# The second attention of a fused two-layer block, rewritten: queries and keys stacked along the partitions, heads' keys packed in chunks, all batches unrolled

## Chip, cores and metric

The kernel runs on one NeuronCore of a Trainium2 chip. The metric is the device time of one launch in microseconds. Three runs of the kernel before the change gave 1285.15, 1285.19 and 1286.05 us; the median is 1285.19 us.

## What is computed

Sixteen batches of 256 tokens by 256 channels (x) pass through two layers. Each layer is a cross attention on a context of 77 rows, and then a feed-forward part. The change is in the second attention:

```
x = x + L0_xattn(layernorm(x), ctx)      # 16 heads of 64, shared key and value, causal
x = x + L0_ffn(layernorm(x))
x = x + L1_xattn(layernorm(x), ctx)      # 16 heads of 16
x = x + L1_ffn(layernorm(x))             # soft mixture of 16 experts

# L1_xattn(x_q, x_kv):
q = x_q @ w_q;  k, v = split(x_kv @ w_kv)          # 16 heads of 16 channels
logits = q.k * 16**-0.5 + (query position - key position) * w_rel[head]
out = softmax(logits) @ v                          # per head, over 77 keys
return out @ w_proj
```

All is fp32. For a product that has to be exact to fp32, an operand is split into a rounded part (`_hi`, of type fp32r) and the rest (`_lo`), and three matmuls (hi·hi, hi·lo, lo·hi) replace one.

## The kernel before

The program is written by hand for each engine; semaphores order the engines, and each engine runs its own list in order. The stages follow one another with a barrier between them: `prologue` (keys and values of both layers from the context, for all batches, kept in SBUF), `attention(0)`, `ffn`, `attention(1)`, `moe`.

`attention` (line 328) serves both layers. For the second one a batch has 8 steps t, one for a pair of heads. GpSimd lays the keys of the batch out so that each head's 16 channels stand on their own partitions with zeros elsewhere (`lay_out_keys`, L733), and the values too (`lay_out_values`, L745 and L747). In step t, TensorE computes the scores of the pair for both halves of the queries: for each half a bf16 matmul that adds the position bias (L484) and an fp32 matmul of 128 x 154 (L486), which the trace shows as two records. VectorE takes the row maxima (`find_maxima`, L641), ScalarE the exponentials (L610), VectorE the sums and inverses (L646, L651), and GpSimd multiplies them (L770). A step later in the same batch loop, for the batch before, TensorE transposes the pair's 2 x 2 blocks of probabilities (L496, four transposes, each of 128 columns of which 77 are a head's keys), ScalarE and VectorE split them (L588, L674), and TensorE weighs the values (L510, six matmuls). In the last part of a batch the heads are projected (L522) and added to x (L684), and the next batch's x is transposed (L451) and multiplied by the query weights (L462). The batches 2 to 14 are one hardware loop (`loop`, L405), and its body has two batches in flight.

SyncE (SP) issues nothing within a batch. Its work in this stage is at the start: three loads of constants and six small copies from SBUF to SBUF that bring the bias rows to their partitions (L427 to L434).

Of the kernel before, what the change touches and what calls it, by code (L numbers as in the profile page):

```python
# [117 lines left out]
def prologue(nc, d, st):  # L118
# [9 lines left out]
    with ExitStack() as stack:  # L128
# [22 lines left out]
        def _(sp):  # L151
# [71 lines left out]
        def _(act):  # L223
# [6 lines left out]
            for t, (out, lo, hi) in enumerate(((wk[0][:, :, 0:DK0], 0, DK0), (wk[0][:, :, DK0:P], 0, DK0),  # L230
# [12 lines left out]
            for g in range(GROUPS):  # L243
                if g < GROUPS - 1:
                    transposed_ctx(g + 1)
                for k in range(G):
                    act.wait_ge(val_psum, g * G + k + 1)
                    nc.scalar.copy(st.val0[0:SK, bass.ds(g * G + k, 1), :], val_ps[k % 2][0:SK, 0:DK0].unsqueeze(1))
                    nc.scalar.copy(st.val1[0:SK, bass.ds(g * G + k, 1), :],
                                   val_ps[k % 2][0:SK, DK0:VC].unsqueeze(1)).then_inc(val_done, 1)  # L250

        @block.vector
        def _(dve):
            for t, (i, a, b, lo, hi) in enumerate(((wk, 0, DK0, 0, DK0), (wk, DK0, P, 0, DK0),
# [4 lines left out]
                op = nc.vector.tensor_tensor(i[1][:, :, a:b], w_raw[:, :, lo:hi], fp32_of(i[0][:, :, a:b]), ALU.subtract)  # L259
# [68 lines left out]
def attention(nc, d, st, index):  # L328
# [6 lines left out]
    with ExitStack() as stack:  # L335
        m = Memory(nc, stack, f"att{index}")
        L0 = index == 0
        dk = DK0 if L0 else DK1
# [13 lines left out]
        KC = 1 if L0 else CH  # L352
        KH = 2 if L0 else HC
# [6 lines left out]
        vals = m.split("vals", [P, (2 if L0 else H) * P + HC * dk])  # L360
# [8 lines left out]
        if L0:  # L369
            ident16 = m.sb("ident16", [P, P], BF16)  # L370
            causal_raw = m.sb("causal_raw", [P, PAIR])
            causal16 = m.sb("causal16", [P, PAIR], BF16)
        else:

            pos_raw = m.sb("pos_raw", [P, N])
            pos16 = m.sb("pos16", [P, N], BF16)

            w_rel = m.sb("w_rel", [H, 1])
            neg_k = m.sb("neg_k", [H, SK])
            slope = m.sb("slope", [H, 2, SK])  # L380
            part = m.sb("part", [H, 2, SK])
            part16 = m.sb("part16", [H, 3, 2, SK], BF16)
            bias16 = m.sb("bias16", [P, H, SK], BF16)

# [7 lines left out]
        bias_in, vals_zero = m.sem("bias_in"), m.sem("vals_zero")  # L392
        c_in, c_ready, zeroed, c_step = m.sem("c_in"), m.sem("c_ready"), m.sem("zeroed"), m.sem("c_step")
# [48 lines left out]
        def _(pe):  # L442
# [1207 lines left out]
```

## Time and profile before

| | us |
|---|---|
| median of three runs | 1285.19 |
| profiled execution, from its first to its last instruction (span) | 1284.3 |
| TensorE busy | 1155.0 (90%) |
| VectorE busy | 946.6 (74%) |
| ScalarE busy | 744.9 (58%) |
| GpSimd busy | 443.5 (35%) |
| DMA traffic | 18.63 MB, mean 15 GB/s |

The device time of the profiled execution itself is not given beside its span. The span is 0.9 us below the median of the runs, and the prediction adds these 0.9 us to a span to get a time. Times within the profile are counted from the first instruction. Busy time is a union of an engine's instructions, so it can't tell alone whether the engine is the bound: for that one looks at what it waited for. The names in the rows leave out the index of the stage and of the buffer, so `att_s_bank` stands for both attentions; the second attention is the stretch from 696.7 to 1032.3 us.

### The profile page before, as it was taken

What the parts mean: (1) busy time and instruction counts of PE and PEld (TensorE: products, weight loads), DVE (VectorE), ACT (ScalarE), POOL (GpSimd) and SP (SyncE); (2) the same over time, 40 slices, a digit from 0 to 9 for tenths busy, and PEclk for the clock granted to TensorE, in tenths of its full rate; (3) what the DMA queues carried; (4) which work ended last, traced back from release to release, by engine and by line L of the source; (5) the groups of instructions that cost most, each with busy time, mean ns of one, the idle gap of its engine ahead of it and who ended that gap; (6) DMA issues with size and microseconds to landing.
All of it is one profiled execution on the core that took longest, in us unless ns stands there. A gap on an engine that the chain in (4) does not pass through costs nothing. (4 is left out here: it accounts for less than half of the span.)

```text
span 1284.3 us, 31779 instructions
## 1 busy us (share of the span) xinstructions
PE 1155.0 (90%) x9045; PEld 1104.0 (86%) x9045; DVE 946.6 (74%) x2439; ACT 744.9 (58%) x2297; POOL 443.5 (35%) x656
## 2 busy tenths in 40 slices
PE   7689999999999987999996799999999947767998
PEld 7689999999999987999996699999999837767777
DVE  3567777677776666777776688888888659997656
ACT  3466677567765654333332577677677516666754
POOL 0232222322322210221213454554555346664015
PEclk9889999999999998999998799999999968999559
DMA  7010000000000001000000000000000000000103
GB/s 239 23 67 1 0 0 0 0 0 0 0 0 0 0 2 29 1 0 0 0 0 4 2 1 0 0 0 0 0 0 0 1 18 1 1 0 1 39 27 123
DMA packets 20583, 18.63 MB, mean 15 GB/s; under 512 B 6620, under 2 KB 19644, under 8 KB 20412
## 3 DMA queue, kind: packets, MB, share of 16 engines
q1 hardware_dynamic: 19724, 17.45, 4.3%
q10 hardware_dynamic: 816, 0.66, 0.2%
q8 instruction: 21, 0.34, 0.1%
q14 instruction: 22, 0.18, 0.0%
HBM read 13.89 MB, written 4.19 MB: 14 GB/s over the span
## 5 line engine op out<-in xcount | busy, mean ns | idle before, releaser
L770 POOL TENSOR_TENSOR att_prob<-att_ex,att_rinv 128x308 f32<-128x308 f32 x256 | 179.8, 705 | 326.1 <-DVE att_rinv L651 290.6
L610 ACT ACTIVATE att_ex<-att_s_bank,att_mx 128x77 f32<-128x77 f32 x1024 | 250.2, 334 | 17.1 <-DVE att_mx L641 15.2
L674 DVE TENSOR_TENSOR att_pT_lo<-att_t_bank,att_pT_hi 128x512 fp32r<-128x512 f32 x256 | 176.6, 690 | 50.4 <-ACT att_pT_hi L588 48.1
L486 PE MATMUL att_s_bank<-att_keys,att_qT 128*128 128x154 f32 x1024 | 205.5, 315 | 0.0
L588 ACT CAST att_pT_hi<-att_t_bank 128x512 fp32r<-128x512 f32 x256 | 150.0, 587 | 75.2 <-PE att_t_bank L496 70.3
L510 PE MATMUL att_o_bank<-att_pT_hi,att_vals_hi 128*128 128x256 f32 x512 | 167.5, 327 | 5.1 <-DVE att_pT_lo L674 2.9
L486 PEld LDWEIGHTS att_s_bank<-att_keys,att_qT 128*128 128x128 f32 x1024 | 152.7, 194 | 6.7
L496 PE MATMUL att_t_bank<-all_ident,att_prob 128*128 128x128 f32 x1024 | 152.9, 272 | 0.0
L510 PE MATMUL att_o_bank<-att_pT_lo,att_vals_hi 128*128 128x256 f32 x512 | 144.1, 281 | 0.0
L510 PE MATMUL att_o_bank<-att_pT_hi,att_vals_lo 128*128 128x256 f32 x512 | 143.9, 281 | 0.0
L618 ACT ACTIVATE att_qT<-att_q_bank 128x256 f32<-128x256 f32 x160 | 61.6, 385 | 136.9 <-PE att_q_bank L462 135.9
L893 ACT ACTIVATE ffn_hid<-ffn_h_bank,ffn_b 128x256 f32<-128x256 f32 x128 | 60.7, 476 | 125.6 <-DVE ffn_hT_lo L924 63.0
L641 DVE TENSOR_REDUCE att_mx<-att_s_bank 128x4 f32<-128x308 f32 x256 | 120.0, 469 | 16.8 <-PE att_s_bank L486 16.8
L646 DVE TENSOR_REDUCE att_rsum<-att_ex 128x4 f32<-128x308 f32 x256 | 118.2, 462 | 1.7 <-ACT att_ex L610 1.2
L496 PEld LDWEIGHTS att_t_bank<-all_ident,att_prob 128*128 128x128 f32 x1024 | 118.1, 140 | 0.0
L510 PEld LDWEIGHTS att_o_bank<-att_pT_hi,att_vals_hi 128*128 128x128 f32 x512 | 96.7, 189 | 9.3 <-DVE att_pT_lo L674 6.5
L462 PE MATMUL att_q_bank<-att_xT_hi,att_wq_hi 128*128 128x256 f32 x320 | 96.1, 300 | 4.9 <-DVE att_xT_lo L634 4.9
L655 DVE TENSOR_TENSOR att_oT_lo<-att_o_bank,att_oT_hi 128x256 fp32r<-128x256 f32 x160 | 67.8, 424 | 40.4 <-ACT att_oT_hi L623 36.6
L510 PEld LDWEIGHTS att_o_bank<-att_pT_lo,att_vals_hi 128*128 128x128 f32 x512 | 96.7, 189 | 0.0
L510 PEld LDWEIGHTS att_o_bank<-att_pT_hi,att_vals_lo 128*128 128x128 f32 x512 | 96.3, 188 | 0.0
L462 PE MATMUL att_q_bank<-att_xT_hi,att_wq_lo 128*128 128x256 f32 x320 | 91.9, 287 | 0.0
L462 PE MATMUL att_q_bank<-att_xT_lo,att_wq_hi 128*128 128x256 f32 x320 | 91.5, 286 | 0.0
(215 smaller groups left out, 3363.0 us busy)
## 6 DMA issues: line engine op xcount, KB each, us to landing
all_x<-in_x SPq DMA_DIRECT2D x4, 1024.0 KB, 8.1
out<-comb_y SPq DMA_DIRECT2D x16, 256.0 KB, 2.1
all_raw<-in_L_ffn_w SPq DMA_DIRECT2D x2, 1024.0 KB, 5.8
moe_w_raw<-in_L_ffn_w SPq DMA_DIRECT2D x32, 64.0 KB, 2.1
pro_ctx_in<-in_ctx SPq DMA_DIRECT2D x4, 308.0 KB
all_raw<-in_L_xattn_W_q SPq DMA_DIRECT2D x1, 1024.0 KB, 8.2
all_raw<-in_L_xattn_W_o SPq DMA_DIRECT2D x1, 1024.0 KB, 10.7
pro_w_raw<-in_L_xattn_w_kv ACTq DMA_DIRECT2D x1, 512.0 KB, 4.8
```

The source lines that it names most:

```text
L462: last = nc.tensor.matmul(q_bank[c % 2][:, 0:N], wq[a][:, k, c * P:(c + 1) * P], xT[b][:, k, :], start=n == 0, stop=n == 5)
L486: last = nc.tensor.matmul(out, qT[c % 2][:, q * P:(q + 1) * P], keys[:, kc, h0:h0 + 2, :], start=first, stop=True)
L496: last = nc.tensor.transpose(t_bank[t % 2][:, h * N + q * P:h * N + (q + 1) * P], prob[:, q, (2 * t + h) * SK:(2 * t + h) * SK + P], st.id ...
L510: last = nc.tensor.matmul(o_bank[j % 2][:, 0:N], vals[a][:, v * P:(v + 1) * P], pT[t % 2][b][:, h * N:(h + 1) * N], start=t % PC == 0 and ...
L588: nc.scalar.copy(pT[t % 2][0][:, :], t_bank[t % 2][:, :]).then_inc(pt_hi, 1)
L610: last = nc.scalar.activation(ex[t % RING][:, r, :], s_bank[t % 2][:, r * SK:(r + 1) * SK], ACT.Exp, bias=mx[t % 2][:, r:r + 1])
L618: nc.scalar.mul(qT[c % 2][:, :], q_bank[c % 2][:, 0:N], scale).then_inc(q_ready, 1)
L641: nc.vector.tensor_reduce(mx[t % 2][:, :], s_bank[t % 2][:, 0:NC * PAIR].rearrange("p (r k) -> p r k", k=SK), AX, ALU.max, negate=True).th ...
L646: nc.vector.tensor_reduce(rsum[t % RING][:, :], ex[t % RING][:, :, :], AX, ALU.add).then_inc(sum_ready, 1)
L655: nc.vector.tensor_tensor(oT[1][:, j, :], o_bank[j % 2][:, 0:N], fp32_of(oT[0][:, j, :]), ALU.subtract).then_inc(ot_lo, 1)
L674: nc.vector.tensor_tensor(pT[t % 2][1][:, :], t_bank[t % 2][:, :], fp32_of(pT[t % 2][0][:, :]), ALU.subtract).then_inc(pt_lo, 1)
L770: nc.gpsimd.tensor_tensor(out, e, w, ALU.mult).then_inc(p_ready, 1)
```

## The change

`attention` becomes two functions. `attention0` does what it did for the first layer. `attention1` is new code for the second:

- **Scores.** Queries and keys are kept as stacks: `qs` has the 16 channels of both heads of a pair three times along the partitions (hi, lo, hi; 96 rows) and four rows with positions and ones, `ks` the keys in the same way (hi, hi, lo) and four bias rows. One fp32r matmul over 100 rows replaces the bias matmul and the fp32 matmul. The scale is folded into the key weights in `prologue`.
- **How the stacks get there.** DMAs from SBUF to SBUF, issued by SyncE: per batch 12 for the queries (`load_queries`), 24 for the keys (`load_keys`) and 20 for the values (`load_values`). `lay_out_keys` is gone; `lay_out_values` multiplies the copied values by a mask, in four GpSimd instructions.
- **Probabilities.** The first 64 keys of a pair of heads fill one 128-column chunk, and the last 13 keys of eight heads fill a 104-column chunk. So a batch has five units of four transposes and six value matmuls in place of eight.
- **Order.** All batches are unrolled into stages f = -2 to 17. In stage f run the scores of batch f, the transposes and values of batch f-1 and the projection of batch f-2, and the queries of batch f+1.
- **prologue.** It splits keys and values of the second layer into hi and lo for all batches (two more ScalarE casts per group of four batches, one more VectorE subtraction per batch).

The core of the diff, with eight columns of indent taken away:

```diff
-def attention(nc, d, st, index):
+def attention0(nc, d, st):
...
+def attention1(nc, d, st):
...
+BIAS, ROWS = 96, 100
...
+qs = [m.sb(f"qs{i}", [P, HP, N], F32R) for i in range(2)]
+ks = [m.sb(f"ks{i}", [P, DC, 4, 2, SK], F32R) for i in range(2)]
+vd = [m.split(f"vd{i}", [P, D]) for i in range(2)]
+vt = [m.split(f"vt{i}", [P, D]) for i in range(2)]
+vmain = [m.split(f"vmain{i}", [P, HP * 160]) for i in range(2)]
+vtail = [m.split(f"vtail{i}", [P, DC, P]) for i in range(2)]
...
+prob = m.sb("prob", [P, NC, HP * P])
+tails = [m.sb(f"tails{i}", [P, NC, 2 * TAILS]) for i in range(2)]
+pT = [m.split(f"pT{i}", [P, 2 * N]) for i in range(2)]
...
+QS_DMAS, KS_DMAS, V_DMAS = 12, 24, 20
+VALS = 4
+STAGES = range(-2, B + 2)
+UNIT_AT = {0: 0, 1: 1, 3: 2, 4: 3, 6: 4}
+CHUNKS = {0: (0, 1), 1: (2, 3), 2: (4, 5), 4: (6, 7)}
+TAIL_UNIT = 3
...
+    sp.dma_start(w_rel[:, :], d["L1_xattn_w_rel"].rearrange("a h -> h a")).then_inc(c_in, 16)
+    sp.dma_start(neg_k[:, :], d["neg_k"]).then_inc(c_in, 16)
+    sp.dma_start(pos_raw[BIAS:ROWS, :], d["positions"]).then_inc(c_in, 16)
+    def load_queries(f):
+        i = f % 2
+        sp.wait_ge(q_lo, f + 1)
+        at_least(sp, s_psum, HP * (f - 1))
+        for k, part in enumerate((0, 1, 0)):
+            for r in range(4):
+                sp.dma_start(fp32_of(qs[i][32 * k:32 * k + 32, :, :]).rearrange("p (c r) n -> p c r n", c=DC)[:, :, r, :],
+                             fp32_of(qT[part][32 * r:32 * r + 32, :, :])).then_inc(qs_in[i], 16)
+    def load_keys(f):
+        i = f % 2
+        at_least(sp, s_psum, HP * (f - 1))
+        for k, part in enumerate((0, 0, 1)):
+            for r in range(4):
+                for h in range(2):
+                    a = 32 * r + DK1 * h
+                    sp.dma_start(fp32_of(ks[i][32 * k + DK1 * h:32 * k + DK1 * h + DK1, :, r, h, :]),
+                                 fp32_of(st.key1[part][a:a + DK1, :, f, :])).then_inc(ks_in[i], 16)
+    def load_values(f):
+        i = f % 2
+        at_least(sp, vals_ready, VALS * (f - 1))
+        for part in range(2):
+            v = fp32_of(st.val1[part][:, f, :])
+            for h in range(2):
+                sp.dma_start(fp32_of(vd[i][part][MAIN * h:MAIN * h + MAIN, :]), v[0:MAIN, :]).then_inc(v_in[i], 16)
+            for h in range(8):
+                sp.dma_start(fp32_of(vt[i][part][TAIL * h:TAIL * h + TAIL, :]), v[MAIN:SK, :]).then_inc(v_in[i], 16)
+    load_values(0)
+    sp.wait_ge(ks_zero, 2)
+    load_keys(0)
+    load_keys(1)
+    load_values(1)
+    sp.wait_ge(c_step, 4)
+    for i in range(2):
+        for r in range(2):
+            for part in range(2):
+                row = BIAS + 2 * r + part
+                sp.dma_start(fp32_of(ks[i][row:row + 1, :, :, :, :]).rearrange("p c r h k -> p (c r h) k"),
+                             fp32_of(bias[part][:, r, :])).then_inc(bias_in, 16)
+    for f in range(B):
+        load_queries(f)
+        if 1 <= f < B - 1:
+            load_keys(f + 1)
+            load_values(f + 1)
...
+    def scores(f, t):
+        i = f % 2
+        if t == 0:
+            pe.wait_ge(qs_in[i], 16 * QS_DMAS * (f // 2 + 1))
+            pe.wait_ge(ks_in[i], 16 * KS_DMAS * (f // 2 + 1))
+        if t == 0 and f < 2:
+            pe.wait_ge(bias_in, 128)
+            pe.wait_ge(pos_ready, 2)
+        at_least(pe, ex_ready, HP * f + t - 1)
+        for q in range(NC):
+            last = nc.tensor.matmul(s_bank[t % 2][:, q * PAIR:(q + 1) * PAIR], qs[i][0:ROWS, t, q * P:(q + 1) * P],
+                                    ks[i][0:ROWS, t // 4, t % 4, :, :], start=True, stop=True)
+        last.then_inc(s_psum, 1)
+    def transpose_p(g, u):
+        n = UNITS * g + u
+        pe.wait_ge(p_ready, probs_of(g, u))
+        at_least(pe, pt_lo, n - 1)
+        for j in range(2):
+            for q in range(NC):
+                at = j * N + q * P
+                if u == TAIL_UNIT:
+                    last = nc.tensor.transpose(t_bank[n % 2][0:TAILS, at:at + P],
+                                               tails[g % 2][:, q, j * TAILS:(j + 1) * TAILS], st.ident[:, :])
+                else:
+                    t = CHUNKS[u][j]
+                    last = nc.tensor.transpose(t_bank[n % 2][:, at:at + P],
+                                               prob[:, q, t * P:(t + 1) * P], st.ident[:, :])
...
+    for f in STAGES:
+        for t in range(HP):
+            if here(f):
+                scores(f, t)
+            if here(f - 1) and t in UNIT_AT:
+                transpose_p(f - 1, UNIT_AT[t])
+            if t == 0 and here(f - 2):
+                weigh_values(f - 2, 4)
+            if t == 0 and here(f + 1):
+                transpose_x(f + 1)
+            if t == 2 and here(f + 1):
+                queries(f + 1)
+            if here(f - 1) and t in (2, 3, 5, 6):
+                weigh_values(f - 1, {2: 0, 3: 1, 5: 2, 6: 3}[t])
+            if t == 4 and here(f - 2):
+                project(f - 2)
...
+    def round_queries(f):
+        act.wait_ge(q_psum, f + 1)
+        at_least(act, qs_in[(f - 1) % 2], 16 * QS_DMAS * ((f - 1) // 2 + 1))
+        nc.scalar.copy(qT[0][:, :, :], xq_bank[:, :].rearrange("p (c n) -> p c n", c=DC)).then_inc(q_hi, 1)
...
+    def weigh(f, t):
+        n = HP * f + t
+        pool.wait_ge(inv_ready, n + 1)
+        if f > 0 and t % 2 == 0:
+            pool.wait_ge(t_psum, UNITS * (f - 1) + unit_of(t) + 1)
+        e = ex[t % RING][:, :, :].rearrange("p (q h) k -> p q h k", q=NC)
+        w = rinv[t % RING][:, :].rearrange("p (q h) -> p q h", q=NC).unsqueeze(3)
+        main = prob[:, :, t * P:(t + 1) * P].rearrange("p q (h k) -> p q h k", h=2)
+        tail = tails[f % 2][:, :, t * 2 * TAIL:(t + 1) * 2 * TAIL].rearrange("p q (h k) -> p q h k", h=2)
+        nc.gpsimd.tensor_tensor(main, e[:, :, :, 0:MAIN], w.to_broadcast([P, NC, 2, MAIN]), ALU.mult).then_inc(p_ready, 1)
+        nc.gpsimd.tensor_tensor(tail, e[:, :, :, MAIN:SK], w.to_broadcast([P, NC, 2, TAIL]), ALU.mult).then_inc(p_ready, 1)
...
+        pool.wait_ge(v_in[i], 16 * V_DMAS * (g // 2 + 1))
+        at_least(pool, pv_done, UNITS * (g - 1))
+        for part in range(2):
+            main = vmain[i][part][:, :].rearrange("p (t n) -> p t n", n=160)[:, :, 0:2 * DK1]
...
@@ prologue
-        for j in range(3):
-            dve.wait_ge(key_psum, g * 3 + j + 1)
...
-            nc.vector.tensor_copy(out, keys).then_inc(key_done, 1)
...
+        for k in range(G):
+            dve.wait_ge(val1_hi, g * G + k + 1)
+            nc.vector.tensor_tensor(st.val1[1][0:SK, bass.ds(g * G + k, 1), :],
+                                    val_ps[k % 2][0:SK, DK0:VC].unsqueeze(1),
+                                    fp32_of(st.val1[0][0:SK, bass.ds(g * G + k, 1), :]), ALU.subtract).then_inc(val_done, 1)
```

The list of SyncE at the start of the second attention, before (the names are destination<-source, then the shape of the destination):

```order
L427 DMA att_w_rel<-in_L_xattn_w_rel 16x1
L428 DMA att_neg_k<-in_neg_k 16x77
L429 DMA att_pos_raw<-in_positions 128x256
L434 DMA att_bias<-att_part 1x16x77 x6
```

After these the list before has nothing until the next stage. The same place of the changed kernel, first the rows that stand ahead of the first queries:

```order
L839 DMA att_pos_raw<-in_positions 4x256
L866 DMA att_vd_hi<-kv_val_hi 64x256 x2
L868 DMA att_vt_hi<-kv_val_hi 13x256 x8
L866 DMA att_vd_lo<-kv_val_lo 64x256 x2
L868 DMA att_vt_lo<-kv_val_lo 13x256 x8
L857 DMA att_ks<-kv_key_hi 16x2x77 x16
L857 DMA att_ks<-kv_key_lo 16x2x77 x8
L857 DMA att_ks<-kv_key_hi 16x2x77 x16
L857 DMA att_ks<-kv_key_lo 16x2x77 x8
```

and then, for one batch in the middle of the stage, what SyncE has to issue each time:

```order
L847 DMA att_qs<-att_qT_hi 32x2x256 x4
L847 DMA att_qs<-att_qT_lo 32x2x256 x4
L847 DMA att_qs<-att_qT_hi 32x2x256 x4
L857 DMA att_ks<-kv_key_hi 16x2x77 x16
L857 DMA att_ks<-kv_key_lo 16x2x77 x8
L866 DMA att_vd_hi<-kv_val_hi 64x256 x2
L868 DMA att_vt_hi<-kv_val_hi 13x256 x8
L866 DMA att_vd_lo<-kv_val_lo 64x256 x2
L868 DMA att_vt_lo<-kv_val_lo 13x256 x8
```

These are 12 + 24 + 20 = 56 DMAs; before there were none in a batch. On TensorE, one step of the loop before, for a pair of heads:

```order
L496 MATMUL att_t_bank<-all_ident,att_prob 128x128 x4
L484 MATMUL att_s_bank<-att_bias,att_pos 128x154
L486 MATMUL att_s_bank<-att_keys,att_qT 128x154
L484 MATMUL att_s_bank<-att_bias,att_pos 128x154
L486 MATMUL att_s_bank<-att_keys,att_qT 128x154
L510 MATMUL att_o_bank<-att_pT_hi,att_vals_hi 128x256
L510 MATMUL att_o_bank<-att_pT_lo,att_vals_hi 128x256
L510 MATMUL att_o_bank<-att_pT_hi,att_vals_lo 128x256
L510 MATMUL att_o_bank<-att_pT_hi,att_vals_hi 128x256
L510 MATMUL att_o_bank<-att_pT_lo,att_vals_hi 128x256
L510 MATMUL att_o_bank<-att_pT_hi,att_vals_lo 128x256
```

and in the changed kernel the end of a stage's step t = 0 and its steps t = 1 and 2, as far as the first query matmul:

```order
L961 MATMUL att_o_bank<-att_pT_hi,att_vmain_hi 128x256
L961 MATMUL att_o_bank<-att_pT_lo,att_vmain_hi 128x256
L961 MATMUL att_o_bank<-att_pT_hi,att_vmain_lo 128x256
L900 MATMUL att_xq_bank<-all_ident,att_xn 128x128 x4
L924 MATMUL att_s_bank<-att_ks,att_qs 128x154 x2
L940 MATMUL att_t_bank<-all_ident,att_prob 128x128 x4
L924 MATMUL att_s_bank<-att_ks,att_qs 128x154 x2
L910 MATMUL att_xq_bank<-att_xT_hi,att_wq_hi 128x256
```

Two score matmuls stand where four (six records in the trace) stood, and the scores of a stage's first step wait for the DMAs of `qs` and `ks` (`scores`, t == 0), with all else of that stage behind them on TensorE.

## Rows read from the trace of the kernel before

**Rows 1.** Windows: busy of each engine, start, steady part, last batch; granted clock in shares.

```profile
core 0: us, PE busy (x) PEld busy (x) DVE busy (x) ACT busy (x) POOL busy (x), PEclk, DMA share, GB/s
841.68:860.84 19.16, 18.88 (x159) 18.10 (x157) 16.52 (x45) 13.72 (x46) 10.21 (x17) 1.00 0.00 0
...
708.00:714.00 6.00, 3.62 (x15) 2.88 (x15) 2.08 (x5) 1.13 (x3) 0.00 (x0) 0.50 0.03 4
...
1190.00:1248.00 58.00, 53.86 (x214) 44.47 (x215) 34.90 (x102) 38.67 (x99) 2.55 (x2) 0.50 0.12 32
```

**Rows 2.** Timeline of ScalarE: the same cast in three batches, one per batch.

```profile
841.68 0.65 ACT L578 CAST att_xT_hi<-att_q_bank 128x256 fp32r<-128x256 f32 x2 [0.28 <-PE att_q_bank L451]
...
860.84 0.65 ACT L578 CAST att_xT_hi<-att_q_bank 128x256 fp32r<-128x256 f32 x2 [0.27 <-PE att_q_bank L451]
...
880.01 0.65 ACT L578 CAST att_xT_hi<-att_q_bank 128x256 fp32r<-128x256 f32 x2 [0.26 <-PE att_q_bank L451]
```

**Rows 3.** Timeline of TensorE, one steady step: start, duration, what.

```profile
848.90 0.46 PEld L496 LDWEIGHTS att_t_bank<-all_ident,att_prob 128*128 128x128 f32 x4
...
849.33 0.10 PEld L484 LDWEIGHTS att_s_bank<-att_bias,att_pos 128*128 128x128 bf16 x1
...
850.05 0.19 PEld L510 LDWEIGHTS att_o_bank<-att_pT_hi,att_vals_hi 128*128 128x128 f32 x1
...
850.80 0.46 PEld L496 LDWEIGHTS att_t_bank<-all_ident,att_prob 128*128 128x128 f32 x4
```

**Rows 4.** Groups by line and shape, 725 to 1010 us: busy, mean ns, idle before.

```profile
L674 DVE TENSOR_TENSOR att_pT_lo<-att_t_bank,att_pT_hi 128x512 fp32r<-128x512 f32 x118 | 81.5, 691 | 13.0 <-ACT att_pT_hi L588 11.1
...
L733 POOL TENSOR_TENSOR att_keys<-kv_key,all_head_mask 128x616 f32<-128x616 f32 x30 | 36.7, 1222 | 0.0
```

**Rows 5.** Timeline of SP, start of the program: issues back to back.

```profile
1.22 0.38 SPq L153 DMA_DIRECT2D all_ident<-in_ident  x1
1.65 0.43 SPq L154 DMA_DIRECT2D all_head_mask<-in_head_mask  x1
2.12 0.43 SPq L155 DMA_DIRECT2D all_head_mask<-in_head_mask  x1
...
15.82 0.31 SPq L165 DMA_DIRECT2D pro_ctx_in<-in_ctx  x1
```

**Rows 6.** Timeline of SP in the second attention: all that it issues there.

```profile
696.72 0.35 SPq L427 DMA_DIRECT2D att_w_rel<-in_L_xattn_w_rel  x1
697.12 0.41 SPq L428 DMA_DIRECT2D att_neg_k<-in_neg_k  x1
697.58 0.41 SPq L429 DMA_DIRECT2D att_pos_raw<-in_positions  x1
708.08 3.79 SPq L434 DMA_DIRECT2D att_bias<-att_part  x6
```

**Rows 7.** The six copies of L434: duration min/median/max, first and last start, landing.

```profile
L434 SPq DMA_DIRECT2D att_bias<-att_part x6: 585/589/630, 708.1 to 711.3; - x6
...
DMA to landing us min/median/max: 1.8/1.8/2.1
```

**Rows 8.** Timeline of SP after 1033 us: the first and last of nine back to back.

```profile
1033.26 0.36 SPq L1051 DMA_DIRECT2D route_gamma<-in_L_ffn_ln_gamma  x1
...
1037.72 1.09 SPq L1337 DMA_DIRECT2D moe_w_raw<-in_L_ffn_w  x1
```

**Rows 9.** The line that loads 64x256 floats: duration min/median/max of 16.

```profile
L1337 SPq DMA_DIRECT2D moe_w_raw<-in_L_ffn_w x16: 480/490/1091, 1036.5 to 1231.3; - x16
```

**Rows 10.** Timeline: the first scores, the last batch's first transposes, the last addition.

```profile
713.12 0.29 PE L484 MATMUL att_s_bank<-att_bias,att_pos 128*128 128x154 bf16 x1 [0.68 <-DMA att_bias<-att_part]
...
1017.32 1.04 PE L496 MATMUL att_t_bank<-all_ident,att_prob 128*128 128x128 f32 x8
...
1028.18 0.69 DVE L674 TENSOR_TENSOR att_pT_lo<-att_t_bank,att_pT_hi 128x512 fp32r<-128x512 f32 x1 [0.45 <-ACT att_pT_hi L588]
...
1031.90 0.42 DVE L684 TENSOR_TENSOR all_x<-att_q_bank,all_x 128x256 f32<-128x256 f32 x1
```

**Rows 11.** Part 3 of the page: a queue's packets, MB, share of 16 engines.

```profile
q1 hardware_dynamic: 19724, 17.45, 4.3%
```

**Rows 12.** Groups by line: the casts of the values in the prologue.

```profile
L249 ACT COPY kv_val<-pro_val_ps 77x256 f32<-77x256 f32 x16 | 5.9, 371 | 0.0
```

More of the change, by code:

```diff
@@ L44 @@
 LN_EPS = 1e-5
+MAIN, TAIL = 64, SK - 64
+TAILS = 8 * TAIL
 PASSES = ((0, 0), (0, 1), (1, 0))
@@ L243, in _ @@
             for g in range(GROUPS):
+                for c in range(DC):
+                    act.wait_ge(key_psum, g * 3 + c + 2)
+                    nc.scalar.copy(st.key1[0][:, c, bass.ds(g * G, G), :],
+                                   key_ps[c + 1][:, 0:GK].rearrange("p (b k) -> p b k", b=G)).then_inc(key1_hi, 1)
                 if g < GROUPS - 1:
@@ L258, in _ @@
                 dve.wait_ge(w_hi, t + 1)
-                op = nc.vector.tensor_tensor(i[1][:, :, a:b], w_raw[:, :, lo:hi], fp32_of(i[0][:, :, a:b]), ALU.subtract)
+                if t == 2:
+                    for c in range(DC):
+                        op = nc.vector.scalar_tensor_tensor(i[1][:, c, a:b], w_raw[:, c, lo:hi], DK1 ** -0.5,
+                                                            fp32_of(i[0][:, c, a:b]), ALU.mult, ALU.subtract)
+                else:
+                    op = nc.vector.tensor_tensor(i[1][:, :, a:b], w_raw[:, :, lo:hi], fp32_of(i[0][:, :, a:b]), ALU.subtract)
                 if t == 2:
@@ L368, in attention @@
         oT = m.split("oT", [P, CH, N])
[L369 to L383, printed above, removed]
+        ident16 = m.sb("ident16", [P, P], BF16)
+        causal_raw = m.sb("causal_raw", [P, PAIR])
+        causal16 = m.sb("causal16", [P, PAIR], BF16)
         q_bank = [m.ps(f"q_bank{i}") for i in range(2)]
@@ L477, in scores @@
                     first = True
-                    if L0 and q == 0:
+                    if q == 0:
                         nc.tensor.matmul(out, ident16[:, :], causal16[:, :], start=True, stop=False)
-                        first = False
-                    if not L0:
-                        nc.tensor.matmul(out, pos16[:, q * P:(q + 1) * P], bias16[:, 2 * t:2 * t + 2, :], start=True, stop=False)
                         first = False
@@ L724, in _ @@
             ln.inverse_deviation(pool, 0)
-            if not L0:
-                pool.memset(bias16[:, :, :], 0.0).then_inc(zeroed, 1)
             def lay_out_keys(f, c):
@@ L1604, in build @@
         st.head_mask0 = m.sb("head_mask0", [P, 2])
-        st.head_mask1 = m.sb("head_mask1", [P, 8])
+        st.tail_mask = m.sb("tail_mask", [P, H])
         with ExitStack() as kv_stack:
             kv = Memory(nc, kv_stack, "kv")
-            st.key0 = kv.sb("key0", [P, B, SK])
-            st.key1 = kv.sb("key1", [P, DC, B, SK])
-            st.val0 = kv.sb("val0", [P, B, DK0])
-            st.val1 = kv.sb("val1", [P, B, D])
-            prologue(nc, d, st)
-            attention(nc, d, st, 0)
+            st.key1 = kv.split("key1", [P, DC, B, SK])
+            st.val1 = kv.split("val1", [P, B, D])
+            with ExitStack() as kv0_stack:
+                kv0 = Memory(nc, kv0_stack, "kv0")
+                st.key0 = kv0.sb("key0", [P, B, SK])
+                st.val0 = kv0.sb("val0", [P, B, DK0])
+                prologue(nc, d, st)
+                attention0(nc, d, st)
             ffn(nc, d, st)
-            attention(nc, d, st, 1)
+            attention1(nc, d, st)
         moe(nc, d, st, out)
```

361 lines of the change are left out of this document (295 added, 66 removed).

## The prediction

> **What bounds the kernel now.** I read the windows first, to see which engine fills a batch of the second attention. Between two casts of the same line, 19.17 us apart in each of the batches shown [rows 2], TensorE is busy 18.88 of 19.16 us, VectorE 16.52, ScalarE 13.72 and GpSimd 10.21, at the full granted clock [rows 1]. TensorE never waits long there, so it is the bound, and VectorE is only 2.6 us behind. The timeline then gives TensorE's step for a pair of heads: it starts every 1.90 us, with 0.43 us for four transposes, 0.72 us for the scores and 0.75 us for the values [rows 3]. Eight steps are 15.2 us; the other 4.0 us of a batch are x's transposes, queries and projection. The stage's first scores start at 713.12 us and its last addition begins at 1031.90 and takes 0.42, so it ends at 1032.3 [rows 10]. SyncE's first issue is at 696.72 [rows 6].
>
> Last I read SP's own timeline, because the change puts 56 DMAs per batch on a queue that had none. SP issues one after another, and each issue occupies it: 0.38 and 0.43 us, 0.43 to 0.47 us from start to start [rows 5]; 0.40 and 0.46 us in the second attention [rows 6]; 8 intervals in 4.46 us, 0.56 us each, after 1033 us [rows 8]; the form 64x256, which the values have, takes 0.49 us itself [rows 9]. The only copies from SBUF to SBUF are six of the bias: 0.59 us each in the median, (711.3 - 708.1) / 5 = 0.64 us apart, and landing 1.8 us after issue [rows 7].
>
> **TensorE's saving.** Transposes go from 8 groups of 0.43 us to 5, values from 8 of 0.75 to 5: -3.5 us. The scores were 8 x 0.72 = 5.8 us. No row has an fp32r matmul of 154 columns. At the pace of the value matmuls (0.75 / 6 = 0.125 us, with more columns) 16 of them take 2.0 us; at the pace of now, as if fp32r bought nothing, 5.8. TensorE's batch becomes 11.9 us (up to 15.7). I take 11.9, since the value matmuls have the same type.
>
> **The others.** VectorE loses three subtractions of 0.69 us [rows 4] and gains one for the queries: 16.52 - 1.4 = 15.1 us. GpSimd loses two key layouts of 1.22 us [rows 4] and gets four smaller instructions for values and a second multiplication per pair; it had 9 us free. Nothing here would exceed 16 us, so by the compute engines alone a batch would take about 16 us instead of 19.2.
>
> **What the change adds: 56 issues.** They stand in one list on SP: 12 for the queries of f, then 24 for the keys and 20 for the values of f+1. The first scores of a batch wait for its queries; the queries' copies can't be issued before the keys and values ahead of them in SP's list are. Call c the time from one issue to the next. A batch then takes 56c. To hide behind 19.2 us of work c would have to be 0.34 us, and behind 16 us it would have to be 0.28. The ends for c are 0.36 (the shortest issue, 0.31 us [rows 5], plus the 0.05 us between two) and 0.64 (the bias copies). Below 0.36 no row supports it. The bias copies are nearest in kind, but they gather 16 partitions into one, which the 56 don't do; the loads nearest in shape give 0.47 (plain) and 0.54 (64x256: 0.49 + 0.05). I take the middle, c = 0.50. A batch is then 28.0 us. Waits of SP: q_lo(f) comes about 6.5 us into stage f-1, and SP reaches the queries of f some 20 us into it, so SP doesn't wait in the steady part; the wait of the keys for the scores of the batch before last is long over as well. Two buffers don't help: the list is serial and full.
>
> The DMA engines themselves carry it: 19724 packets took 4.3% of 16 engines' span [rows 11], 45 ns each, and 56 DMAs have 12x64 + 24x32 + 4x64 + 16x13 = 2000 pieces, 2000 x 45 / 16 = 5.6 us per batch.
>
> **The sum**, on the profiled execution's clock:
> - Start: SP issues its three constants until 698.1. Then 88 copies for keys and values of two batches, 44.0 us; 8 bias copies of 0.64, 5.1 us; 12 for the queries, 6.0; landing 1.8. First scores at 755.0 instead of 713.1. The memsets of `ks` and the weights' split lie beside it.
> - Batch 1: its queries wait for q_lo, three steps of 1.9 and a split after the first scores, 761.5; issued by 767.5. The keys of batch 2 wait until the scores of batch 0 are over, seven steps, 768.3; then 44 issues, 22 us: 790.3.
> - Thirteen periods of 28.0 us: the queries of batch 15 start at 1154.3; + 6.0 + 1.8: its scores start at 1162.1.
> - Tail: stage 15 runs free, 8 x 1.9 = 15.2 us. Stage 16 has five units, and the last batch now needs (1032.3 - 1017.3) / 8 = 1.9 us for each of eight [rows 10]: 9.4. Stage 17 is the last values, head, projection and addition, now 4.1 us from 1028.18 on [rows 10]. End at 1190.8 against 1032.3: +158.5 us.
> - Prologue: 16 more subtractions on VectorE, and a bank of the values is released only after a cast (0.37 us [rows 12]) and a subtraction. It lengthens the values by about 0.15 us each, +2 us, of a bound of 0 (under the loads) to 6.
> The later stages are unchanged. Span 1284.3 + 160.5 = 1444.8 us, plus the 0.9 us by which the median lies above the span: 1446 us. Of c the sum depends by 88 + 12 + 44 + 13x56 + 12 = 884 issues: 0.01 us in c is 8.8 us in the kernel.
>
> The Trainium skill (DMA: Bandwidth & Descriptors, "Why a DMA increments its semaphore by 16 and not by 1") gives 512 sequencer cycles for a DMA instruction on chips of this generation, and its first page (Trainium Kernel Development and Optimization, "NeuronCore Architecture") 1.2 GHz for SyncE: an estimate of 0.43 us, by which the sum would be 1384 us. The back-to-back rows of 0.43 to 0.47 agree with it roughly, the bias rows don't.
>
> **TensorE's clock** falls in two stretches: 0.50 at the stage's start, where TensorE had stood, and 0.50 also in the experts, although busy 53.86 of 58 us [rows 1]. With 12 of 28 us busy I expect stretches at 1.2 GHz. At that level the 11.9 us of a batch become 24, still below 28; had the scores cost their upper end, 15.7 would be 31 and the batches would take 3 us more: about +45 us.
>
> **Rivals.**
> - *Issues are cheap, compute bounds (faster).* If short copies with fixed addresses take SP under 0.317 us, the kernel is faster, since (1446 - 1285) / 884 = 0.183 below 0.50 is where the gain begins; from 0.28 down VectorE sets the pace. At c = 0.25 the first scores are at about 730, fifteen stages of 16 us follow, the tail adds 29: 999 instead of 1032, 1255 us with the prologue. For it: one isolated issue of 0.31. Against it: it was isolated, and the closest pair shown is 0.40 us apart [rows 6]. The Trainium skill (same page, "Issuing engines are not separate DMA queues") calls an issuer's time usually small relative to the DMA itself; by that rule this rival is the one to expect. The trace doesn't agree: 0.59 us of issue stand against 1.8 us to landing [rows 7]. Chance 0.07.
> - *Short issues, still the bound.* c from 0.32 to 0.39, as the isolated issues of 0.31 to 0.35 plus the gap: at 0.36, 1322 us. Chance 0.10.
> - *All copies cost like the bias copies.* c = 0.64, 35.8 us per batch: 1446 + 884 x 0.14 = 1570 us. For it: they are the only rows from SBUF to SBUF, the first of them took 0.63 us after a pause, and in the run of nine an issue took 1.09 [rows 8], so a long list may be slower than a short one. Chance 0.08.
>
> **Numbers.** My forecast, SP's list as the bound with c between 0.39 and 0.63, has 0.75. The range is from c = 0.39 (1349) to the neighbourhood of 0.63 (1561), with TensorE's clock within it: 1350 to 1560. A measurement of this kernel tells 0.2%, 2.6 us, from no change. Faster by more: 0.07. Within it c would have to be 0.314 to 0.320: 0.01. Slower: the rest, 0.75 + 0.10 + 0.08 less that 0.01, 0.92. The range leaves out the low rival for the most part, the faster one and half of the high one.
>
> **What would show it.** SP in the second attention: some 900 issues from end to end without a wait from 698 us to about 1160; TensorE waiting at each first scores for `qs`, 10 us or more per batch; a period of 56 issues, the same batch after batch; PE's clock below 1 there; scores' matmuls at half of before. I am wrong if SP waits in its list for q_lo or for the scores, or if its issues are under 0.32 us, and wrong in size if they are not about 0.50.

## The result, and the profile after

| | before | after |
|---|---|---|
| median | 1285.17 us (4 runs) | 1624.99 us (4 runs, 1623.41 to 1627.62) |
| ratio | | 1.264, 95% interval 1.262 to 1.266 |
| span of the profiled execution | 1284.3 us | 1621.3 us |
| second attention: SyncE's first issue to the end of the last addition | 696.7 to 1032.3 | 699.3 to 1370.6 |
| from there to the last instruction | 252.0 | 250.7 |

The forecast was 1446 us, in 1350 to 1560. The direction and the mechanism were right; the size was not, and the time lies 65 us above the range.

The page of the changed kernel, its parts 1 to 3 (slices of 40.5 us; digits are tenths):

```profile
PE 1070.3 (66%) x8053; PEld 1021.8 (63%) x8053; DVE 924.2 (57%) x2388; ACT 715.6 (44%) x2225; POOL 440.0 (27%) x754
...
PE   7699999999997999930433333333333336677898
...
DVE  4576767777667777740533333333333335899756
...
PEclk9799999999998999965666666666666667799859
...
q1 hardware_dynamic: 65220, 41.38, 9.9%
```

From slice 20 to 33 TensorE and VectorE are busy for about a third of the time. The copies' queue fills 9.9% of 16 engines, against 4.3% before [rows 11], and the engines are 17% busy in the batch shown below, so the transfers themselves have room. The chain of waits on the page is of no help here, since it covers only the last 2% of the span. The waits of the stretch 690 to 1400 us say who waits for whom (waiting group, what it waited for: us, times, longest):

```profile
POOL att_prob L1148 <- DVE att_rinv L1089: 480.6, 76, 61.7
...
PE att_s_bank L924 <- DMA att_qs<-att_qT_hi: 412.3, 16, 58.6
DVE att_mx L1077 <- PE att_s_bank L924: 398.5, 47, 55.2
```

GpSimd waits for VectorE, VectorE for TensorE's scores, TensorE for the copies of the queries, once per batch. So TensorE's wait is the one to follow: to SP, which issues those copies. Its timeline over one batch (start, duration):

```profile
1002.17 5.04 SPq L857 DMA_DIRECT2D att_ks<-kv_key_lo  x8
1007.25 1.23 SPq L866 DMA_DIRECT2D att_vd_hi<-kv_val_hi  x2
1008.52 6.43 SPq L868 DMA_DIRECT2D att_vt_hi<-kv_val_hi  x8
1015.00 1.17 SPq L866 DMA_DIRECT2D att_vd_lo<-kv_val_lo  x2
1016.21 6.36 SPq L868 DMA_DIRECT2D att_vt_lo<-kv_val_lo  x8
1022.68 2.66 SPq L847 DMA_DIRECT2D att_qs<-att_qT_hi  x4
1025.39 2.51 SPq L847 DMA_DIRECT2D att_qs<-att_qT_lo  x4
1027.94 2.51 SPq L847 DMA_DIRECT2D att_qs<-att_qT_hi  x4
1030.50 10.45 SPq L857 DMA_DIRECT2D att_ks<-kv_key_hi  x16
```

One row ends where the next begins, 0.04 to 0.11 us apart: SP doesn't rest in the batch. Its only long wait in the stage is for the queries of batch 1 (us, times, longest):

```profile
SPq L847 <- DVE att_qT_lo L1070: 11.2, 1, 11.2
```

Queries take 7.8 us for 12, keys 10.45 + 5.04 + 0.04 = 15.5 for 24, the two pairs of 64-partition value copies 2.5 for 4, and the 16 copies of 13 partitions 12.9, which is 0.80 each. The same two kinds over the whole stage (duration in ns, min/median/max):

```profile
L857 SPq DMA_DIRECT2D att_ks<-kv_key_hi x256: 586/593/1719, 716.4 to 1313.9; - x128
```

```profile
L868 SPq DMA_DIRECT2D att_vt_hi<-kv_val_hi x128: 743/743/923, 701.7 to 1326.5; - x128
```

ScalarE's cast of x, which had a period of 19.17 us before [rows 2], is at 838.75 and, nine batches on, at 1192.03: 39.25 us, or 0.70 us per issue. The window shows what the compute engines do in such a batch (columns: window, us, PE, PEld, DVE, ACT, POOL busy, granted clock, DMA share, GB/s):

```profile
814.50:853.75 39.25, 13.62 (x94) 12.91 (x94) 14.77 (x40) 11.72 (x41) 9.95 (x22) 0.63 0.17 39
```

Against [rows 1] the change did save work: VectorE 14.77 us a batch instead of 16.52, and TensorE 13.62 although its granted clock was 0.63, between its levels of 1.2 and 2.4 GHz. It saved it on engines that then stood still for 24 us.

The ends of the stretch, on TensorE and VectorE:

```profile
777.26 0.71 PE L924 MATMUL att_s_bank<-att_ks,att_qs 100*128 100x154 f32 x2 [58.56 <-DMA att_qs<-att_qT_hi]
```

```profile
1344.27 0.71 PE L924 MATMUL att_s_bank<-att_ks,att_qs 100*128 100x154 f32 x2 [22.90 <-DMA att_qs<-att_qT_hi]
```

```profile
1369.95 0.69 DVE L1106 TENSOR_TENSOR all_x<-att_proj_bank,all_x 128x512 f32<-128x512 f32 x1 [1.78 <-PE att_proj_bank L973]
```

The first is [rows 10]'s 713.12, 64 us later; the second is the first score matmul of batch 15.

### The profile page after: what moved, and what is told of

The parts are those of the page before. It is cut to its first block and busy times, and to the rows that moved or that the text cites. A ratio compares the mean times of both kernels' runs of the same rounds, so it can differ in the third digit from the quotient of the medians.

```text
span 1621.3 us, 28906 instructions
## 1 busy us (share of the span) xinstructions
PE 1070.3 (66%) x8053; PEld 1021.8 (63%) x8053; DVE 924.2 (57%) x2388; ACT 715.6 (44%) x2225; POOL 440.0 (27%) x754
## 5 line engine op out<-in xcount | busy, mean ns | idle before, releaser
L924 PE MATMUL att_s_bank<-att_ks,att_qs 100*128 100x154 f32 x256 | 59.0, 317 | 426.8 <-DMA att_qs<-att_qT_hi 412.3
L1148 POOL TENSOR_TENSOR att_prob<-att_ex,att_rinv 128x256 f32<-128x256 f32 x128 | 79.4, 620 | 480.8 <-DVE att_rinv L1089 480.6
L740 POOL TENSOR_TENSOR att_prob<-att_ex,att_rinv 128x308 f32<-128x308 f32 x128 | 90.0, 703 | 216.2 <-DVE att_rinv L644 202.9
L667 DVE TENSOR_TENSOR att_pT_lo<-att_t_bank,att_pT_hi 128x512 fp32r<-128x512 f32 x128 | 88.3, 690 | 32.3 <-ACT att_pT_hi L581 32.0
L481 PE MATMUL att_s_bank<-att_keys,att_qT 128*128 128x154 f32 x512 | 95.2, 309 | 0.0
L581 ACT CAST att_pT_hi<-att_t_bank 128x512 fp32r<-128x512 f32 x128 | 75.0, 587 | 24.2 <-PE att_t_bank L491 19.3
L505 PE MATMUL att_o_bank<-att_pT_hi,att_vals_hi 128*128 128x256 f32 x256 | 83.0, 324 | 3.0 <-DVE att_oT_lo L648 2.0
L1263 PE MATMUL ffn_o_bank<-ffn_w_hi,ffn_hT_hi 128*128 128x256 f32 x256 | 74.4, 291 | 8.0 <-DVE ffn_hT_lo L1323 8.0
L491 PE MATMUL att_t_bank<-all_ident,att_prob 128*128 128x128 f32 x512 | 76.5, 272 | 0.0
L1250 PE MATMUL ffn_h_bank<-ffn_xT_hi,ffn_w_hi 128*128 128x256 f32 x256 | 72.6, 283 | 3.5 <-DVE ffn_xT_lo L1310 3.5
L481 PEld LDWEIGHTS att_s_bank<-att_keys,att_qT 128*128 128x128 f32 x512 | 73.5, 194 | 1.0
```

The source lines that it names most:

```text
L481: last = nc.tensor.matmul(out, qT[c % 2][:, q * P:(q + 1) * P], keys[:, kc, h0:h0 + 2, :], start=first, stop=True)
L491: last = nc.tensor.transpose(t_bank[t % 2][:, h * N + q * P:h * N + (q + 1) * P], prob[:, q, (2 * t + h) * SK:(2 * t + h) * SK + P], st.id ...
L505: last = nc.tensor.matmul(o_bank[j % 2][:, 0:N], vals[a][:, v * P:(v + 1) * P], pT[t % 2][b][:, h * N:(h + 1) * N], start=t % PC == 0 and ...
L581: nc.scalar.copy(pT[t % 2][0][:, :], t_bank[t % 2][:, :]).then_inc(pt_hi, 1)
L667: nc.vector.tensor_tensor(pT[t % 2][1][:, :], t_bank[t % 2][:, :], fp32_of(pT[t % 2][0][:, :]), ALU.subtract).then_inc(pt_lo, 1)
L740: nc.gpsimd.tensor_tensor(out, e, w, ALU.mult).then_inc(p_ready, 1)
```

## The experiments

Two theories stood against each other. **A**: the time of an issue depends on the kind of copy; copies from SBUF to SBUF are dear (0.64 us), those of 13 partitions dearer, and SP's serial list of them is the whole loss. **B**: each issue costs about what the loads do, and something else (a full list, the DMA engines, the work on the other side) holds SP up. Where one time is given below, the kernel was run once; repeated runs of one kernel lay within 0.5% of each other, and the differences that are read from such times are about 3% and more.

### Issue times by themselves

The kernel before, with twelve groups of eight copies added on SP in the first attention, where it has nothing to do. Each group is another kind:

```diff
+for j in range(8):
+    sp.dma_start(pr[32:45, j, :], st.ident[0:13, :]).then_inc(pr_sem, 16)
+sp.wait_ge(pr_sem, 640)
```

> The kernel before, with twelve groups of eight copies added to SyncE's list in the first attention, where it has nothing to do; each group is issued back to back and waited for before the next. They copy rows of 512 bytes: from SBUF to SBUF over 128, 64, 32, 16, 13 and 8 partitions, from DRAM to SBUF over 128, 16 and 13, from SBUF to DRAM over 16 and 13, from DRAM to DRAM over 16. The time of the kernel should stay within 0.3% of the kernel before. Theory A (SBUF at both ends makes an issue dear): about 0.59 us per issue for every group from SBUF to SBUF, with 0.74 us at 13 partitions, and 0.38 to 0.45 us where one end is DRAM. Rival B (few partitions make it dear, whichever memories): 0.41 us at 128 and 64 partitions from SBUF to SBUF, 0.59 us at 16 and fewer, and the same 0.59 us from DRAM at 16 partitions. The 13 partitions cost 0.15 us more than 16 in each kind if the count of partitions that share no large factor with 16 is what costs, and only from SBUF to SBUF if it is tied to that kind.

Measured: 1283.25 us, so the additions lie beside other work. SP's timeline, of which the groups of 128, 16 and 13 partitions stand here, SBUF to SBUF; then DRAM to SBUF with 128, 16 and 13; then SBUF to DRAM and DRAM to DRAM with 16:

```profile
73.86 5.07 SPq L444 DMA_DIRECT2D att_pr<-all_ident  x8
...
93.75 4.95 SPq L453 DMA_DIRECT2D att_pr<-all_ident  x8
99.83 6.69 SPq L456 DMA_DIRECT2D att_pr<-all_ident  x8
...
114.74 4.73 SPq L462 DMA_DIRECT2D att_pr<-in_ident  x8
120.94 3.58 SPq L465 DMA_DIRECT2D att_pr<-in_ident  x8
125.89 3.18 SPq L468 DMA_DIRECT2D att_pr<-in_ident  x8
130.23 3.56 SPq L471 DMA_DIRECT2D probe_dram<-all_ident  x8
...
138.97 5.01 SPq L477 DMA_DIRECT2D probe_dram<-in_ident  x8
```

A row of eight has seven gaps in it, so 4.95 us are 0.62 each and 3.58 us 0.45. SBUF to SBUF is 0.64 for 128 partitions and 0.62 for 16, and 0.84 for 13, where one of the eight took 1.05 us and the median is 0.74. For 8 partitions the median duration is 0.625 us, against 0.589 for 16. From DRAM with 128 partitions the median is 0.43, though one of the eight took 1.48 us, so that their row is 4.73 long. Between DRAM and SBUF, either way, it is 0.45 for 16 partitions and 0.40 for 13. In the stage, the sum of 12 x 0.64, 24 x 0.65, 4 x 0.62 and 16 x 0.80 is 38.6 us of the 39.25; the single issues of up to 1.7 us can cover the rest. Outside the stage the same kinds cost about as much, 0.62 to 0.64 and, by the median of 0.743 and a gap of 0.06, 0.80. So theory A's prices hold with short lists and other work around them, and B's "about what the loads do" is out, and so is the rival in the expectation (few partitions alone make an issue dear), since 128 partitions cost 0.64.

One row fits nothing that I had expected: DRAM to DRAM costs 0.63 too. In these twelve groups the dear ones have both ends in the same kind of memory. That isn't a general rule: the strided loads from DRAM in the version through DRAM below take 0.60 us and more as well. What makes an issue dear stays open.

### Keys and values only once

The changed kernel, with the keys and values of batches 0 and 1 alone; the later batches use these again, so the copies of 14 batches are left out of the computation. SP's list falls from 56 to 12 a batch.

```diff
 for f in range(B):
     load_queries(f)
-    if 1 <= f < B - 1:
-        load_keys(f + 1)
-        load_values(f + 1)
```

> The changed kernel with the copies of keys and values left out from the third batch on (all later batches use those of the first two, so keys and values of the other batches are left out of the result); the copies of the queries stay. SyncE then has 12 issues per batch, 7.7 us. Theory (SyncE's list bounds the stage): the first scores stay at 777 us, the period falls from about 39 us to 16 us, the stage ends near 777 + 15 x 16 + 28 = 1045 us and the span is near 1296 us; SyncE waits in each batch. Rival (the new order of work, or TensorE's lower granted clock, is slow by itself): the period stays above 25 us, span above 1430 us.

Measured: 1360.52 us, with a span of 1358.4 where 1296 was expected. The copies of keys and values are worth 264 us. This run alone doesn't tell the time of the issues from that of the transfers; the next two do. And the period fell only to 19 to 21.5 us, where the compute engines were expected to reach 16. TensorE's wait from 800 to 1000 us, and SP's in the stage, which now comes in 15 batches:

```profile
PE att_s_bank L921 <- DMA att_qs<-att_qT_hi: 51.4, 10, 6.0
...
SPq L847 <- DVE att_qT_lo L1067: 182.0, 15, 13.0
```

TensorE still waits 5.1 us in each batch for the queries, with SP free. This wait has another cause: x is cast at the start of stage f, the queries of f+1 are multiplied, rounded and split, then copied by 12 issues (7.7 us) and land 2 us later, all of it before the first scores of stage f+1.

### Tail rows in 16 partitions instead of 13

The changed kernel, with each group of 13 value rows copied as 16 (three more rows, multiplied by zeros), so the same 56 issues with more bytes.

```diff
-sp.dma_start(fp32_of(vt[i][part][TAIL * h:TAIL * h + TAIL, :]), v[MAIN:SK, :]).then_inc(v_in[i], 16)
+sp.dma_start(fp32_of(vt[i][part][TPAD * h:TPAD * h + TPAD, :]), v[SK - TPAD:SK, :]).then_inc(v_in[i], 16)
```

> The changed kernel with the sixteen tail copies per batch made over 16 partitions (keys 61 to 76) instead of 13, three of them weighed with zero; count of copies and order as before, more bytes. Theory (issue time of SyncE counts, and 13 partitions cost 0.74 us instead of 0.59): the period falls by 16 x 0.15 = 2.4 us, the stage by (32 + 14 x 16) x 0.15 = 38 us, to a span near 1583 us. Rival (bytes or landings count): no change or a little slower, 1621 us or more.

Measured: 1578.03 us, 47 less than the changed kernel (a span of 1575.9, near 1583 expected), and a period of 36.7 us (two casts of x); then the issues of these copies:

```profile
830.55 0.58 ACT L1000 CAST att_xT_hi<-att_xq_bank 128x512 fp32r<-128x512 f32 x1 [0.48 <-PE att_xq_bank L902]
867.22 0.58 ACT L1000 CAST att_xT_hi<-att_xq_bank 128x512 fp32r<-128x512 f32 x1 [0.48 <-PE att_xq_bank L902]
...
L870 SPq DMA_DIRECT2D att_vt_hi<-kv_val_hi x128: 585/589/1573, 701.9 to 1282.9; - x128
```

More bytes in less time: the issue takes 0.589 us in the median instead of 0.743, and 16 of them in a batch give 2.5 of the 2.6 us by which the period fell. The rival that bytes or landings count, which wanted 1621 us or more, is out.

### The tail copies issued by ScalarE

The changed kernel, with the same 56 copies a batch, but the 16 of 13 partitions issued by ScalarE, two in each step, for batches 2 to 15. This keeps the bytes and the number of copies and changes only who issues.

```diff
+def load_tail(f, h):
+    i = f % 2
+    for part in range(2):
+        act.dma_start(fp32_of(vt[i][part][TAIL * h:TAIL * h + TAIL, :]),
+                      fp32_of(st.val1[part][:, f, :])[MAIN:SK, :]).then_inc(v_in[i], 16)
```

> Edit: the changed kernel, with the 16 copies of the 13-partition value rows of a batch issued from ScalarE (2 in each of the eight head-pair steps), for batches 2 to 15; same copies, same bytes, same 56 a batch, another sequencer. Theory (the issuing engine's serial time bounds, not what the copies do to the DMA engines): SyncE's list is 12 x 0.64 + 24 x 0.635 + 4 x 0.62 = 25.4 us a batch, ScalarE's work 11.7 + 16 x 0.74 = 23.5 us; the period falls from 39.25 to 26 to 28 us, so 14 x 12 = about 165 us less: about 1460 us (1440 to 1490). Rival (the copies themselves, or one path that all issues share, whatever engine they come from, take 0.70 us each): the period stays near 39 us and the time near 1625 us; between the two, where issues of two engines disturb one another, the durations of L866 and of the ScalarE issues rise above 0.75 us.

Measured: 1468.96 us, period 28.1 us. The expected time was about 1460. SP is left with 40 issues, 28.1 / 40 = 0.70 each, where 0.635 was reckoned; ScalarE's issues and SP's copies of `key_lo` show a part of why:

```profile
L1031 ACTq DMA_DIRECT2D att_vt_hi<-kv_val_hi x112: 777/777/1388, 799.0 to 1179.4; - x112
```

```profile
L857 SPq DMA_DIRECT2D att_ks<-kv_key_lo x128: 585/645/1180, 727.5 to 1176.0; - x128
```

SP's issue of `key_lo` has a median of 0.645 us instead of 0.592, 9% more beside ScalarE's issues, while that of `key_hi` stays at 0.593. Single issues of up to 1.6 us can be the rest. ScalarE's own take 0.777 where SP's took 0.743; whether that is the other engine or the two at once, no run tells. But they work side by side. The issuing engine's own time is the bound, and not a path that all issues share.

### Through DRAM

A version of the change with few issues. Keys and values are stored to DRAM once, in the first attention where SP is idle; per batch 10 loads bring them back, and the queries take 2 stores and 3 loads: 15 issues instead of 56.

```diff
+sp.dma_start(st.qd[0][f], fp32_of(qT[0][:, :, :])).then_inc(q_out, 16)
...
+for k, part in enumerate((0, 1, 0)):
+    sp.dma_start(fp32_of(qs[i][32 * k:32 * k + 32, :, :]).rearrange("p (c r) n -> p c r n", c=DC),
+                 st.qd[part][f].rearrange("(r p) c n -> p c r n", r=4)).then_inc(qs_in[i], 16)
```

> The changed kernel with the same matmuls and the same stacks, but filled from DRAM: keys and values are stored to DRAM once during the first attention (22 stores), the queries of a batch are stored in two stores and read back in three loads, keys take six loads and values four: 15 DMAs per batch instead of 56, each with DRAM at one end. Theory: about 0.42 us per issue, 6.5 us of SyncE per batch, so that VectorE bounds: period 16 us, first scores near 717 us, the stage ends near 717 + 15 x 16 + 28 = 985 us instead of 1032 in the kernel before: 1240 us in all, faster than both. Rival: the two landings in series (store, then load, about 2 us each) between the queries and the next batch's scores set the period, 19 us or more: 1285 us or above.

Measured: 1294.41 us (1293.70 to 1298.94), ratio to before 1.007, interval 1.005 to 1.009. 331 us of the 340 are gone, but the kernel is still behind the one before: the 1240 us expected are missed, and the rival in the expectation (two landings in series set the period) is what came. In the batch from 846.63 to 866.82 us, TensorE's first scores and SP's list:

```profile
842.89 0.71 PE L932 MATMUL att_s_bank<-att_ks,att_qs 100*128 100x154 f32 x2 [4.79 <-DMA att_qs<-qd]
```

```profile
852.39 0.33 SPq L853 DMA_DIRECT2D qd<-att_qT_hi  x1
854.45 0.32 SPq L855 DMA_DIRECT2D qd<-att_qT_lo  x1
856.55 1.88 SPq L859 DMA_DIRECT2D att_qs<-qd  x3
...
L859 SPq DMA_DIRECT2D att_qs<-qd x48: 568/613/1256, 722.5 to 1012.4; - x48
L868 SPq DMA_DIRECT2D att_ks<-kd x96: 555/601/727, 702.7 to 998.2; - x96
```

The store is at 854.45, its landing releases the loads at 856.55, and those land by about 863: the chain of a batch's queries, and not the length of SP's list, sets this period of 18 to 20 us. It is the same wait as with the keys copied once.

The last two rows correct the price that was expected, "about 0.42 us per issue". These loads gather strided rows from DRAM, and their issues take 0.61 and 0.60 us, as much as the copies from SBUF to SBUF, while the two stores take 0.33 and 0.32. The 15 issues of a batch take about 8 us of SP instead of 6.5. So the version gains by having fewer issues, and hardly by having cheaper ones.

### The queries one stage earlier

The last kernel, with transposes, queries, rounding and stores of batch f+2 in stage f (LayerNorm of f+3), so that the chain has a whole stage more.

```diff
-if t == 0 and here(f + 1):
-    transpose_x(f + 1)
-if t == 2 and here(f + 1):
-    queries(f + 1)
+if t == 0 and here(f + 2):
+    transpose_x(f + 2)
+if t == 2 and here(f + 2):
+    queries(f + 2)
```

> Edit: the kernel of e4 (keys and values written to DRAM once, queries by 2 stores and 3 loads), and each batch's queries made one stage earlier, so that in stage f batch f + 2's queries are computed and stored and batch f + 1's are only loaded. Still 15 issues a batch. Theory (two things hold the period up in turn: the 56 issues of SyncE, and once they are gone the chain cast, query matmuls, store, load, next scores, which took the whole 18.3 to 20.3 us period of e4): the PE wait for the stacked queries, 4.79 us in e4's batch, goes, and the period falls to VectorE's work, 14.3 to 15.1 us a batch, plus its short waits: 16 to 17 us. Against e4 that is 16 x (19.4 - 16.5) = 46 us less: 1294.4 - 46 = about 1248 us, in 1235 to 1262, faster than before's 1285.2. Rival (the compute part itself needs 18 to 20 us a batch, by hand-offs between TensorE, VectorE, ScalarE and GpSimd, and the wait for the queries only covers it): the period stays at 18 to 20 us and the time at 1285 to 1300 us.

Measured: 1258.87 us (1256.99 to 1261.29, five runs; 1248 expected, in 1235 to 1262), ratio to before 0.979, interval 0.978 to 0.981: faster than both kernels, by 2% against the one before. The period is 17.1 us; the window of one batch, and SP's list in it, which now has rests of 1 to 4 us between the stores and the loads:

```profile
834.60:851.70 17.10, 14.08 (x96) 13.17 (x95) 14.55 (x41) 11.53 (x41) 9.94 (x23) 0.80 0.48 120
```

```profile
840.36 0.33 SPq L852 DMA_DIRECT2D qd<-att_qT_hi  x1
842.19 0.32 SPq L854 DMA_DIRECT2D qd<-att_qT_lo  x1
846.33 1.88 SPq L861 DMA_DIRECT2D att_qs<-qd  x3
848.25 3.83 SPq L870 DMA_DIRECT2D att_ks<-kd  x6
```

The wait for the queries is gone from TensorE. What is left of it, over the whole stage:

```profile
PE att_s_bank L937 <- ACT att_ex L1024: 39.6, 38, 2.6
...
PE att_xq_bank L913 <- DVE att_xn L351: 15.1, 14, 4.1
```

That is hand-offs between engines, 2.5 and 0.9 us a batch, and no longer a transfer. The rival, that compute itself needs 18 to 20 us, is out.

## Why the prediction failed in size

- **The mechanism held.** SP issued from 700.5 to 1342.8 us and waited once for longer than 1 us, 11.2 us for the queries of batch 1 (the forecast had such a wait too, of 8.3 us), TensorE waited at every first score (412.3 us, 16 times), the period repeated, and TensorE's clock was below 1.
- **The step that failed is "I take the middle, c = 0.50".** The bias rows (0.64) were the only copies from SBUF to SBUF [rows 7], and I gave them half the weight, because they gather partitions and the 56 don't. The first experiment shows that plain copies from SBUF to SBUF, which gather nothing, cost 0.62 to 0.64 with 16 partitions as with 128. For the copies of 13 partitions even the upper end was too low: 0.80. The mean is 0.70, and 884 x 0.20 = 177 us.
- **The same, by stretch** (forecast with the 2 us for the prologue): first scores 777.3 instead of 757.0, +20; from there to the first scores of batch 15, 567.0 us instead of 407.1, +160, of which 13 x (39.25 - 28.0) = 146 are the periods, 9 the first 44 issues after the queries of batch 1 (31.1 instead of 22), and 4 the queries of batch 1 themselves, whose q_lo came 9.7 us after the first scores and not 6.5; tail 26.3 instead of 28.7, -2. The later stages gave -1.3, and the median stands 3.7 us above the span where 0.9 was added, +2.8. In all 179 us.
- **The two ends.** The rival with c = 0.64 came nearest (1570), and got 0.08. It was also short, since it took one price for two kinds. The upper end for c was the dearest kind of copy in the trace, while a form without any row (13 partitions) was in the list 16 times a batch.
- **The estimate of 0.43 us** by the Trainium skill (DMA: Bandwidth & Descriptors, "Why a DMA increments its semaphore by 16 and not by 1") is met by the plain copies between DRAM and SBUF of the first experiment, 0.40 to 0.45 from start to start. It is not met from SBUF to SBUF (0.62 to 0.80), nor from DRAM to DRAM (0.63), nor by the strided loads from DRAM (0.60 and 0.61 in the median, without the gap). The rule of the same page ("Issuing engines are not separate DMA queues"), that an issuer's time is usually small relative to the DMA, does not hold in this case: 0.64 and 0.80 us against 1.8 to 2.0 to landing, 56 times over.
- **The compute terms.** VectorE's 15.1 us were 14.77. TensorE's scores cost 0.18 us for two matmuls where its clock was full (the last experiment, below, from 840.32 to 840.50), 0.09 each and not the 0.125 taken: the upper end of 5.8 us a batch was far off. The 11.9 us of a whole batch at the full clock were not measured, since the granted clock was 0.63 to 0.80 in the batches of every version looked at. "About 16 us by the compute engines alone" was 17.1 in the best version, and 18 to 21 in two others, for a reason that the prediction did not have: the chain of the queries through a transfer, which the long list had hidden. Where I had costed the faster rival at fifteen stages of 16 us and 1255 us, this chain would have been in its way. (By its own terms that sum comes to 1254.)

```profile
840.32 0.35 PE L937 MATMUL att_s_bank<-att_ks,att_qs 100*128 100x154 f32 x2
840.50 0.61 PE L953 MATMUL att_t_bank<-all_ident,att_prob 128*128 128x128 f32 x4
```

- **Prologue and clock.** SyncE's first issue in the stage came 2.5 us later, 2 were forecast. The clock of 0.63 cost nothing in the batches, since SP's list had no rest in them: with 13.6 of 39 us busy there was room, as said. The DMA engines' 5.6 us a batch were about 6.7 (0.17 of 39.25).

## What to carry to other kernels

Before a layout is made by DMAs, count the issues per period and price each kind by a row of the same form (its two ends, its partitions, its strides): at 0.6 to 0.8 us each, thirty small copies fill the issuing engine for 20 us, however few bytes they move. Where many are needed, a pass through DRAM with few, large, strided loads does the same in a quarter of the issues, though each such load costs 0.6 us as well; and then the latency of two landings in series must be paid by work one stage ahead. If a price ranges over a factor of two and the sum hangs on it nearly alone, take the row of the same kind rather than the middle, and let the range reach past it for forms that have no row.

## What the runs showed of the hardware that was not expected

- An issue from DRAM to DRAM took 0.59 us in the median, like SBUF to SBUF, against 0.42 to 0.43 for 16 or 128 partitions between the two. But loads of strided rows from DRAM took 0.60 and 0.61, so the two memories alone don't give the price.
- 13 partitions cost 0.15 us more than 16 where both ends are in SBUF (0.743 against 0.589), and 0.05 less where one is in DRAM (0.368 against 0.420).
- An issue can take far longer than its form explains. In the last experiment's first attention, 22 large stores follow one another. The store of the keys' rounded part took 0.43 us to issue as the first in the list, and the same store of the rest 2.70 in the middle of it; the stores of 64 partitions took 0.72 to 2.99 us, those of 13 partitions 1.13 to 6.52:

```profile
41.61 0.43 SPq L437 DMA_DIRECT2D kd<-kv_key_hi  x1
42.08 2.43 SPq L440 DMA_DIRECT2D vdd<-kv_val_hi  x2
44.55 25.47 SPq L442 DMA_DIRECT2D vtd<-kv_val_hi  x8
70.06 2.70 SPq L437 DMA_DIRECT2D kd<-kv_key_lo  x1
72.81 5.25 SPq L440 DMA_DIRECT2D vdd<-kv_val_lo  x2
```

The DMA engines were 73 to 80% busy from 41 to 78 us, against 17% in a batch of the changed kernel. That the stores already under way hold SP up there fits these numbers; no run tried it. Why small copies of 13 partitions are dearer than those of 16 from SBUF to SBUF was not tried further either, and stays open.
